# Moving the softmax exponential between two halves of ScalarE's copies, with a one-column exponential behind the gate

## The reference, cut to what matters

```python
hmid = gelu(gate_in @ gate_w1.T + gate_b1)
logits = (hmid @ gate_w2.T + base_bias).reshape(B, L, H, 4) / temp
probs = softmax(logits, -1)
probs = maximum(probs, floor); probs = probs / probs.sum(-1)
out = sum(probs[..., i] * paths[i])     # short FIR, long FIR, delta, v
```

## Time and profile before

| | us |
|---|---|
| median of the runs | 1926.37 |
| lowest, highest run | 1919.24, 2399.18 |
| the profiled execution | 1926.54 |
| its span, first to last instruction | 1924.8 |

### The profile page before, as it was taken

One profiled execution on the slowest core, in us unless ns is written; L12 is line 12 of the kernel. 1 busy time (PEld: TensorE's weight loads), 2 busy tenths in 40 slices (PEclk: granted clock), 3 DMA queues, 4 the chain that ended last, 5 costly groups with the idle time before them and its releaser, 6 DMA issues. The chain is left out here.

```text
span 1924.8 us, 40883 instructions
## 1 busy us (share of the span) xinstructions
PE 1521.7 (79%) x12507; PEld 1127.7 (59%) x12508; DVE 1351.6 (70%) x3875; ACT 951.2 (49%) x1990; POOL 437.7 (23%) x473
## 2 busy tenths in 40 slices
PE   6776075879999999999999999997535999999800
PEld 3446044746747747657657567476234888888700
DVE  7996055778788887887887887886446455554488
ACT  6771160355455554654654555551442555555434
POOL 6783200000030030040030120300314333333300
PEclk9997595988999999999999999988757999999955
DMA  6548832022243153233333342333614633333295
GB/s 203 187 163 241 188 67 53 12 70 70 79 117 94 55 131 100 56 109 99 81 85 99 97 112 77 76 90 87 198 66 138 199 105 102 102 105 100 80 372 195
DMA packets 297373, 224.36 MB, mean 117 GB/s; under 512 B 173472, under 2 KB 265632, under 8 KB 296960
## 3 DMA queue, kind: packets, MB, share of 16 engines
q1 hardware_dynamic: 225600, 158.84, 29.2%
q0 software_dynamic: 15232, 43.53, 6.3%
q10 hardware_dynamic: 56384, 19.93, 4.4%
HBM read 130.42 MB, written 91.82 MB: 115 GB/s over the span
## 5 line engine op out<-in xcount | busy, mean ns | idle before, releaser
L2035 POOL DMA_INDIRECT y_d<-C_yb,C_dest x136 | 131.7, 968 | 234.9 <-ACT C_yb L2146 232.5
L1459 DVE SCALAR_TENSOR_TENSOR B_conv<-B_ps_x,B_cw,B_conv 128x511 f32<-128x511 f32 (+2 forms) x192 | 143.3, 747 | 42.6 <-ACT B_conv L1177 37.6
L688 POOL MEMSET B_z<- 128x256 f32 (+4 forms) x40 | 6.3, 215 | 716.7 <-DMA B_z<-scr_a 716.7
L422 POOL DMA_INDIRECT xs_d<-x,slot_u x128 | 133.3, 1042 | 134.0 <-DVE m_acc L1861 97.2
L2265 DVE TENSOR_TENSOR C_av<-C_sg,C_ps_g 128x256 f32<-128x256 f32 x136 | 57.3, 421 | 94.9 <-ACT C_sg L2140 94.9
L1177 ACT ACTIVATE B_conv<-B_ps_x,B_cw 128x512 f32<-128x512 f32 x64 | 43.8, 685 | 161.3 <-PE B_ps_x L745 159.8
L745 PE MATMUL B_ps_x<-B_xa,B_wk 128*128 128x512 f32 x128 | 68.2, 660 | 67.4 <-DVE B_sel L1451 44.8
L2069 PE MATMUL C_ps_g<-C_w_high,C_xt_high 128*128 x272 | 120.0, 441 | 0.3 <-issue 0.3
L2277 DVE TENSOR_TENSOR C_avt_low<-C_ps_a,C_avt_high 128x256 fp32r<-128x256 f32 x136 | 57.8, 425 | 84.4 <-ACT C_avt_high L2135 84.4
L2069 PE MATMUL C_ps_g<-C_w_high,C_xt_low 128*128 x272 | 108.2, 398 | 0.0
L2069 PE MATMUL C_ps_g<-C_w_low,C_xt_high 128*128 x272 | 107.4, 395 | 0.0
(11 more groups left out here) (333 smaller groups left out, 4366.0 us busy)
## 6 DMA issues: line engine op xcount, KB each, us to landing
C_xb<-xs_d SPq DMA_DIRECT2D x136, 132.0 KB, 2.1
C_w_high<-y_d SPq DMA_DIRECT2D x12, 1024.0 KB, 14.0
A_band<-fir_long POOLq DMA_DIRECT2D x32, 256.0 KB, 5.4
A_work<-xT SPq DMA_DIRECT2D x16, 512.0 KB, 5.0
v_d<-A_v_tok SPq DMA_DIRECT2D x16, 512.0 KB, 3.5
short_d<-A_sh_tok SPq DMA_DIRECT2D x16, 512.0 KB, 3.2
B_xa<-xT SPq DMA_DIRECT2D x8, 1024.0 KB, 5.8
B_v_tok<-v_d SPq DMA_DIRECT2D x8, 1024.0 KB, 5.7
```

Of the source, the lines that this page charges most:

```text
L422: pool.indirect_dma_start(t["xs_d"][:, :], bass.IndirectOffsetOnAxis(ap=slot_u[:, c:c + 1], axis=0), x1[:, b, j, :], None).then_inc(done, 16)
L1459: V.scalar_tensor_tensor(conv[:, g % 2, k:], X[g % 2][:, :SEQ - k], cw[:, g // 4, gg % CH, 3 - k:4 - k], conv[:, g % 2, k:], ALU.mult, ALU ...
L2035: pool.indirect_dma_start(t["y_d"][:, :], bass.IndirectOffsetOnAxis(ap=dest[:, q:q + 1], axis=0), yb[:, u], None).then_inc(y_out[u], 16)
```

## The change

On ScalarE only. `keep_at` can now copy a part of its eight banks. The wait for VectorE's four operations and the exponential leave the head of `merge_and_mix` and become `exponentials(i)`, which stands behind the fourth of the eight copies. Directly behind the gate, ahead of the first copy, ScalarE computes the exponential of a one-column tile into a new one-column tile `warm` that nobody reads. The DMAs of `load_solved` stay behind the eighth copy.

```diff
-        eps6 = sb("eps6", [P, 1]); eps5 = sb("eps5", [P, 1])
+        eps6 = sb("eps6", [P, 1]); eps5 = sb("eps5", [P, 1]); warm = sb("warm", [P, 1])
...
-                def keep_at(p):
-                    for n_ in range(PT):
+                def keep_at(p, first, last):
+                    for n_ in range(first, last):
...
+                def exponentials(i):
+                    act.wait_ge(sm_dve, 11 * i + 4)
+                    A(lg[:], lg[:], ACT.Exp).then_inc(sm_exp, 1)
...
                 def merge_and_mix(i, has_next, has_after):
-                    act.wait_ge(sm_dve, 11 * i + 4)
-                    A(lg[:], lg[:], ACT.Exp).then_inc(sm_exp, 1)
                     if has_next:
                         load_solved(i + 1)
...
-                keep_at(0)
+                keep_at(0, 0, PT)
...
                     for b in range(2):
                         gate(i, b)
-                    if has_next:
-                        keep_at(i + 1)
+                    A(warm[:], eps5[:], ACT.Exp)
+                    if has_next:
+                        keep_at(i + 1, 0, PT // 2)
+                    exponentials(i)
+                    if has_next:
+                        keep_at(i + 1, PT // 2, PT)
                     merge_and_mix(i, has_next, has_after)
```

## The result

| | before | after |
|---|---|---|
| median of the runs, us | 1923.99 | 1898.39 |
| lowest, highest run of after, us | | 1892.64, 1904.81 |
| profiled execution, us | 1926.5 | 1897.1 |
| its span, us | 1924.8 | 1895.4 |
| mean granted clock | 0.888 | 0.899 |

The prediction said 1917.2 us and a range down to 1908. It was wrong: the gain is nearly three times the 9.3 us of its sum.

What follows compares the result with a forecast made beforehand. TensorE was busiest (79%); VectorE's 29.1 us wait for the exponential was the ceiling for direct gain. 0 x 5 + 6.9 + 2.4 = 9.3 us off 1926.5 us gave 1917.2 us, range 1908 to 1927.

Steps and rivals of the forecast that it cites:

- the 9.3 us of its sum: Whole kernel: 0 for each of steps 1 to 5, 6.9 us for step 0, 2.4 us for step 6.
- The one-column exponential and the load: ScalarE ahead of the copies: 1.28 us load, up to 0.31 us exponential, hidden by 0.6 us of cover; cost 0.
- Rival 4: Second group of `at_rest`: the load ahead of the copies makes TensorE wait; slower, 1943 us; chance 0.06.
- VectorE's lead: Steps 1 to 5: VectorE goes on 3.6 us earlier; ScalarE's 1177 leaves 1.8 us, GpSimd's mask leaves nothing.
- the sign that the prediction named for it: Steps 1 to 5: products 937 would stand as far behind the exponential's operands as before.
- Steps 0 and 6: Where VectorE's lateness reaches TensorE at products 898: gains of 6.9 us in step 0 and 2.4 us in step 6.
- The first 3.84 us: Step 0, products 898: TensorE's idling for VectorE goes, as they follow the idle matmuls; 3.84 us gained.
- The other 3.05 us: Step 0, products 898 to 937: VectorE early enough, so 19.5 us as in step 2 instead of 22.6 us.
- the end of 4.3: Step 6, upper end: 2.6 us, and 1.7 us more if products 937 also get the upper clock.
- Gain of steps 1 to 5: 0: Steps 1 to 5: line 1729 still ends 1.08 us behind GpSimd's mask, so nothing is gained; 0 us.
- rival 1: Line 1729 gets past GpSimd's mask, 1.8 us earlier; steps 1 and 3 shed 4.7 us, 1912.5 us; chance 0.12.
- Rival 2: VectorE's whole wait for the exponential is gained, 7 x 3.6 = 25 us, 1901 us; chance 0.02.

Runs made afterwards that it cites:

- e18: Kernel before, with the unused one-column tile and one idle matmul in TensorE's wait ahead of products 937; 1901.98 us, ratio 0.9899.
- e16: Changed kernel with one idle matmul in TensorE's wait for VectorE ahead of products 937, second timing; 1891.81 us, ratio 0.982.
- e13: Kernel before with only the unused one-column tile added, second timing; 1919.57 us, ratio 0.9971.
- e12: Changed kernel with one idle matmul in TensorE's wait for VectorE ahead of products 937, first timing; 1894.94 us, ratio 0.9831.
- e14: Changed kernel with its new tile allocated behind all others, so no address moves, second timing; 1912.01 us, ratio 0.9934.
- e15: Changed kernel, nothing altered, timed once more; 1901.01 us, ratio 0.9884 to the kernel before.
- e17: Kernel before with one idle matmul in TensorE's wait ahead of products 937, nothing else; 1911.46 us, ratio 0.9925.
- e9: Changed kernel with every tile that a DMA touches back at its old place modulo 256, except `xf`; 1907.10 us, ratio 0.9892.

## Why the prediction was wrong

**What held.** The one-column exponential and the load: the load took 1.28 us, the exponential 0.20 us (0.31 was taken), and the second group of `at_rest` did not wait. ScalarE waited 0.15 us for the operands. Rival 4 did not come. Nor is there the drain with which the Trainium skill (ScalarE: Activation LUTs, What ACT_TABLE_LOAD costs) would have made the copies late: in all eight steps the load starts 0.02 us behind the copy of the raw logits, and `warm` 0.01 us behind the load's end.

**VectorE's lead.** It was eaten where the prediction said. Part goes to ScalarE's 1177: idle time before 1465 in steps 1 to 5 is 24.3 us after and was 16.5. Part goes to the mask: ten products of line 1735 take 17.8 us where ten of 1729 took 12.3, and in each of steps 1 to 5 it ends 1.07 or 1.08 us behind the mask, forecast 1.08. But the sign that the prediction named for it, 937 as far behind the exponential's operands as before, did not come: 33.0 to 33.5 us in steps 1 to 5, where it was 34.1 to 35.9. The groups of VectorE's lines over steps 1 to 5 (busy us, mean ns, idle us before them and what ended most of it), after:

```profile
L1465 DVE SCALAR_TENSOR_TENSOR B_conv<-B_ps_x,B_cw,B_conv 128x511 f32<-128x511 f32 (+2 forms) x120 | 89.6, 747 | 24.3 <-ACT B_conv L1177 21.3
L1735 DVE TENSOR_TENSOR B_lo<-B_lo,B_delta 128x1024 f32<-128x1024 f32 x10 | 17.8, 1775 | 0.3
```

and before:

```profile
L1459 DVE SCALAR_TENSOR_TENSOR B_conv<-B_ps_x,B_cw,B_conv 128x511 f32<-128x511 f32 (+2 forms) x120 | 89.5, 746 | 16.5 <-ACT B_conv L1177 13.5
L1729 DVE TENSOR_TENSOR B_lo<-B_lo,B_delta 128x1024 f32<-128x1024 f32 x10 | 12.3, 1235 | 0.3
```

The exclusion of VectorE and GpSimd that the Trainium skill states (SBUF — State Buffer, Who interferes with whom) is seen again in 4.59 us of step 6.

**Steps 0 and 6: right in size, in part for another reason.** Step 0 gave 6.95 us against 6.9. The first 3.84 us are VectorE's wait, as forecast. The other 3.05 us were put down to VectorE being early enough behind it, but they are the clock: products 898, the idle matmuls and products 905 took 3.28, 3.78 and 2.38 us behind the wait and take 2.21, 1.98 and 2.21 us now, which is 3.04 us, and the stretch at the lower level is gone. The forecast took its 19.5 us from a step in which these ran at the upper clock, and so had this part right in size without the reason: that is luck. Step 6 gave 3.5 against 2.4, within the end of 4.3, also by another course: 1.1 us is the DMA's wait ahead of 882 (1.66 to 0.53 us), 1.6 us the clock behind it (products 882 2.59 to 2.21 us, the eight idle records 4.90 to 3.70 us), 1.0 us the wait of 898, as forecast, and from 898 to 937 it lost 0.3 us instead of gaining 1.4; 1735 met the mask's start there. The pair e18 and e16, which differ by the change's instructions, gives 6.7 us in step 0 (130.55 to 123.87 us) and 2.1 us in step 6 (132.65 to 130.59 us), together 8.7 us; here too e18 has 6.8 us at the lower level behind the wait of 3.84 us and e16 has none. So the sum of 9.3 us is not a price at a fixed clock: some 3 us of it, in step 0, are the clock.

**The step that failed: "Gain of steps 1 to 5: 0".** Two things were left out of it.

1. *TensorE's clock was taken as fixed.* The row was in hand: 937 with 3.67 us behind a wait of 1.48 us and a clock of 0.50 behind it. It was used to bound rival 1 for two steps, by the length of that instruction alone. What it costs is read from e13 and e18, which differ by the idle matmul: steps 1 to 5 take 683.2 and 663.1 us, with 44.4 us and none at the lower level, so 0.45 us for each us there. These two differ in their waits as well; but over steps 1 to 5 of all 20 profiled executions the 21 steps without any lower level take 132.1 us on average, the 30 with 3.4 us there 133.4 and the 21 with some 10 us 136.2, and a straight line through all 100 steps rises by 0.44 us for each us. The change took 30.7 us of it away: 30.7 x 0.45 = 13.8 of the 17.1 us, an estimate. That leaves 3.3 us for the shorter waits themselves, VectorE's and the DMA's; steps with no lower clock bear it out, 132.6 us in e18 against 131.6 to 132.1 in e12 and e16. Rival 1 named this step, but priced it at 4.7 us.
2. *The tile was costed at nothing*, since nobody reads it. It moved the tiles behind it, the DMAs of line 609 landed 1.1 us earlier, and 882's wait went from 5.9 to 0.5 us over steps 1 to 6. Alone that is worth 4 and 6 us, under the early exponential 11 us (e14 against e15), and it was part of no rival.

**Rival 2** (the whole wait gained, 1901 us) named a time near the result with a cause that the runs refute: its evidence against, that 898 had no idle time, was right.

**What stays open.** Moving the exponential with no address moved (e14) gave 13.7 us, of which 8.9 us in steps 1 to 5, where 34.1 us at the lower level stand against 51.2; yet the wait ahead of 937, 6.0 us over six steps, is the same as before. That the wait ahead of 937 carries the larger part of the lower clock is shown by e17 and e18, which fill it (10.2 and 0 us at the lower level in steps 1 to 5). Why the clock falls less often behind a wait of the same length when VectorE or the DMA is earlier elsewhere is not shown. Nor is it shown which tile beside `xf` carries the other half of the shift.

## What to carry to other kernels

Cost a change first at a fixed clock, wait by wait, and take no length from a row at another clock; then look at TensorE's granted clock behind each of its waits and price the stretch, not the one instruction, for a wait of about one us may cost more behind it than in itself, and one idle matmul in it may give as much as the move of the producer. A new tile is an edit of every address behind it: keep the addresses fixed when an instruction is to be judged, and try the shift by itself. Two small effects and their sum are to be timed beside each other, with enough rounds that the excess can be told from spread; six to ten runs of each did not do it here.

## What was not expected of the hardware

- A 32-byte shift of tiles, from 224 to 0 modulo 256, shortened the median landing of DMAs from 4.5 to 3.4 us, also of DMAs that don't touch the tile that mattered (e9, 3.3 us). By the Trainium skill (DMA: Bandwidth & Descriptors, How a descriptor splits into AXI transactions) a descriptor that starts off a 256-byte boundary costs extra transfer beats; the section tells it of reads, and the direction agrees with the numbers here, where `xf` is written.
- TensorE's clock decided more than VectorE's wait: with one idle matmul ahead of each 937 the granted clock is 1.00 over 663 us (e18, with the tile) against 0.96 over 683 us before, and an edit that adds work gives 15 us (e17), and 14 to 18 us more beside the tile (e18 against e13). The Trainium skill (TensorE: Matmul & The Clock Gate, The HAM clock gate) says that the clock follows how busy the array has been; the pair of rows of 937, 3.67 us and 1.99 us, agrees.
- An early VectorE instruction can be the dearer one: 1735 took 1.23 us where it started behind the mask, 2.26 us inside it and 4.59 us at its start (step 6).
